# Fire attention: weights, transposes and output steps moved to later slots of the pipeline

## The chip, the cores and the metric

The kernel runs on one core of a Trainium2 chip. A core has five engines that run side by side and are tied together only by semaphores: TensorE (PE: matmuls; PEld is its loading of stationary operands), VectorE (DVE), ScalarE (ACT), GpSimd (POOL) and SyncE (SP, which issues transfers). The metric is the device time of one execution in microseconds; less is better.

## The reference

The reference runs two layers of a "macaron" network on x of 8 x 256 tokens with 128 channels, in float32: a mixture of experts, a gated linear recurrence and the mixture again, then six layers of local attention, one attention with a FIRE position bias, and the six local layers again. Each part starts from a layer norm and its output is added to x. The change touches the FIRE attention alone:

```python
qkv = x @ Wqkv + bqkv
q, k, v = jnp.split(qkv, 3, axis=-1)      # 16 heads of 8 channels each
bias = fire_bias(T, w1, b1, w2, b2, c_param, L_multiplier)   # (1, 16, T, T), -inf above the diagonal
att = jnp.einsum('bhqd,bhkd->bhqk', q, k) * scale + bias
att = jax.nn.softmax(att, axis=-1)
y = jnp.einsum('bhqk,bhkd->bhqd', att, v)
return y.transpose(0, 2, 1, 3).reshape(B, T, C) @ Wproj + bproj
```

## The kernel before

Every phase is written engine by engine: each engine has its own program, executes it strictly in the order written, and waits on semaphores where it needs another engine's result. The phase in question is `fire_attention_phase`. Its first blocks load the constants, build the position bias of both query tiles and the projections q, k, v of the eight batches. Its last block, the attention proper, is what the change rewrites.

The attention is cut into 96 **items**, 12 for each of 8 batches. An item q is one PSUM bank of 128 x 512 scores. Items 0 to 3 of a batch are the first 128 queries: 4 heads by 128 keys each. Items 4 to 11 are the other 128 queries: 2 heads by 256 keys. Items 3 and 11 of a batch end an output **tile** of 128 queries, so there are 16 tiles. Each item goes through these steps:

- `scores` (PE, L1564): four matmuls at once, one for each of the next four items, into banks 0 to 3. Before the next four it waits until the bias has been added to all earlier items (`addd`).
- `add_bias` (DVE, L1663), four in a row as soon as the scores are there, into one of eight buffers S (traced as fa_nd); then `maximum` (DVE, L1670), one a slot.
- subtraction of the maximum (POOL, L1544), in place.
- exponential (ACT, L1639), in place.
- `turn_weights` (PE, L1555): four 128 x 128 transposes into bank 4 or 5, and their copy to pT (ACT, L1633). There are three buffers pT.
- `weigh` (PE, L1592): four matmuls with the values into bank 6 or 7, whose column of ones also gives the sum of the softmax.

A finished tile then takes: copy of heads (ACT, L1627, oh), `turn_heads` (PE, L1580, four transposes), `take_output` (DVE, L1675 and L1679: reciprocal and product, on), `turn_output` (PE, L1575), its copy (ACT, L1645, oT), `project` (PE, L1570), its copy with the bias (ACT, L1651, ysb) and `update` (DVE, L1685, M += ysb).

The order on each engine comes from a software pipeline. The loop `stream` counts slots n, and in slot n an engine does a step for item n - k if the step has lag k:

```python
SIM, PTR, PVS, OTT, OTR, YPR = 0, 2, 3, 4, 5, 6
def stream(slot):
    for n in range(GN + YPR):
        slot(n)
```

So PE's slot n is: turn_weights(n - 2), scores(n) if n is a multiple of 4, project of the tile that ended at n - 6, turn_output (n - 5), turn_heads (n - 4), weigh(n - 3). ACT's slot n is: heads (n - 4), pT (n - 2), exponential of item n, oT (n - 5), ysb (n - 6). DVE's slot n is: four add_bias if n is a multiple of 4, maximum(n), take_output (n - 4), update (n - 6). An exponential is thus written two slots ahead of its transposes. The phase has no loop on the chip and its attention block issues no transfers.

Of the kernel before, what the change touches and what calls it, by code (L numbers as in the profile page):

```python
# [9 lines left out]
ACT = mybir.ActivationFunctionType  # L10
AX = mybir.AxisListType

P = 128
# [1302 lines left out]
def fire_attention_phase(nc, res, d, M, XN):  # L1316

    bank, ident = res["bank"], res["ident"]
# [3 lines left out]
    GN = B * GB  # L1322
    RM = T + 4 * (T // 4 - 1)
    ROFF = RM - T
    with ExitStack() as ctx:
        phase = res["phase"] = res["phase"] + 1

        def sb(name, shape, dt=FP32):
            return ctx.enter_context(nc.sbuf_tensor(f"{name}_{phase}", shape, dt))

        def sem(name):
            s = ctx.enter_context(nc.semaphore(f"{name}_{phase}"))
            sems.append(s)
            return s
        sems = []
        wqkv, wp = sb("fa_wqkv", [P, C]), sb("fa_wp", [P, P])
        bqk, bv = sb("fa_bqk", [P, 3]), sb("fa_bv", [P, P])
# [9 lines left out]
        bias = [sb("fa_bias0", [P, NH, P]), sb("fa_bias1", [P, NH, T])]  # L1347
# [4 lines left out]
        S = nd[:, :, :, :].rearrange("p a i n -> p (a i n)").rearrange("p (g n) -> p g n", g=8)  # L1352
        mx = sb("fa_mx", [P, 8, GR])
        pT = sb("fa_pT", [P, 3, 4, P])
        rd = sb("fa_rd", [P, 2, NH])
        on = sb("fa_on", [P, 2, P])
        oh = sb("fa_oh", [P, 2, 512])
        oT = sb("fa_oT", [P, 2, P])
        ysb = sb("fa_ysb", [P, 2, P])
# [3 lines left out]
        simd, addd, mxd, subd, expd = [sem("fa_" + n) for n in ("simd", "addd", "mxd", "subd", "expd")]  # L1363
        ptT, ptE, pvd = [sem("fa_" + n) for n in ("ptT", "ptE", "pvd")]
        ohE, ohT, rdd, ond, oTd, oTe, yd, yE, upd = [sem("fa_" + n) for n in (
            "ohE", "ohT", "rdd", "ond", "oTd", "oTe", "yd", "yE", "upd")]
        SCALE = float(np.float32(1.0) / np.sqrt(np.float32(HD)))

        with nc.Block() as block:
            @block.sync  # L1370
            def _(sp):
                for dst, src in ((sc[:, 0:2], d["fa_sc"].to_broadcast([P, 2])), (rel[:, :], d["c_rel"]), (pn[:, :], d["c_pos"]),
                                 (wb[:, :], d["fa_wb"]), (wqkv[:, :], d["fa_wqkv"]), (bqk[:, :], d["fa_bqk"]),
                                 (bv[:, :], d["fa_bv"].to_broadcast([P, P])), (b2[:, :], d["fa_b2"].to_broadcast([P, NH])),
                                 (hmask[:, :], d["c_hmask"]), (wp[:, :], d["fa_wp"])):
                    sp.dma_start(dst, src).then_inc(ld, 16)
                sp.wait_ge(zd, 1)
                for g in range(4):
                    sp.dma_start(w2[g * BW:(g + 1) * BW, g * NH:(g + 1) * NH], d["fa_w2"]).then_inc(ld, 16)
                sp.wait_ge(ld, 16 * 14)  # L1380
# [129 lines left out]
                    spread_keys(r)  # L1510
                    forget_future(r)

        SIM, PTR, PVS, OTT, OTR, YPR = 0, 2, 3, 4, 5, 6

        def at(n, k):

            return n - k if 0 <= n - k < GN else None

        def info(q):

            b, i = divmod(q, GB)
            part, r = divmod(i, GR)
            return (b, r, 0, 0, 4, P) if part == 0 else (b, r, 1, 2 * (part - 1), 2, T)

        def tile_end(q):

            if q is None or q % GB not in (GR - 1, GB - 1):
                return None
            return 2 * (q // GB) + (q % GB == GB - 1)

        def stream(slot):
            for n in range(GN + YPR):
                slot(n)

        with nc.Block() as block:
# [13 lines left out]
            def _(pe):  # L1549
# [47 lines left out]
                def slot(n):  # L1597
# [16 lines left out]
                    if q is not None:  # L1614
                        weigh(q)
                stream(slot)

            @block.scalar
            def _(act):
                def slot(n):  # L1620
                    qe = at(n, OTT)
                    tl = tile_end(qe)
                    if tl is not None:
                        act.wait_ge(pvd, qe + 1)
                        if tl >= 2:
                            act.wait_ge(ohT, tl - 1)
                        nc.scalar.activation(oh[:, tl % 2, :], bank[6 + tl % 2][:, :], ACT.Copy).then_inc(ohE, 1)  # L1627
                    q = at(n, PTR)
                    if q is not None:
                        act.wait_ge(ptT, q + 1)  # L1630
                        if q >= 3:
                            act.wait_ge(pvd, q - 2)
                        nc.scalar.activation(pT[:, q % 3, :, :], bank[4 + q % 2][:, :].rearrange("p (h q) -> p h q", h=4),  # L1633
                                             ACT.Copy).then_inc(ptE, 1)
                    q = at(n, SIM)
                    if q is not None:
                        act.wait_ge(subd, q + 1)
                        s = S[:, q % 8, :]
                        nc.scalar.activation(s, s, ACT.Exp).then_inc(expd, 1)  # L1639
                    tl = tile_end(at(n, OTR))  # L1640
                    if tl is not None:
                        act.wait_ge(oTd, tl + 1)
                        if tl >= 2:
                            act.wait_ge(yd, tl - 1)
                        nc.scalar.activation(oT[:, tl % 2, :], bank[6 + tl % 2][:, 0:P], ACT.Copy).then_inc(oTe, 1)  # L1645
                    tl = tile_end(at(n, YPR))
                    if tl is not None:
                        act.wait_ge(yd, tl + 1)
                        if tl >= 2:
                            act.wait_ge(upd, tl - 1)  # L1650
                        nc.scalar.activation(ysb[:, tl % 2, :], bank[6 + tl % 2][:, P:2 * P], ACT.Identity,  # L1651
                                             bias=bqk[:, 2:3]).then_inc(yE, 1)
                stream(slot)

            @block.vector
            def _(dve):
                def add_bias(q):
                    _, r, t, a, nh, nk = info(q)
                    s = S[:, q % 8, :].rearrange("p (h k) -> p h k", h=nh)
                    dve.wait_ge(simd, q + 1)  # L1660
                    if q >= 8:
                        dve.wait_ge(ptT, q - 7)
                    nc.vector.tensor_tensor(s, bank[r][:, :].rearrange("p (h k) -> p h k", h=nh),  # L1663
                                            bias[t][:, 4 * r + a:4 * r + a + nh, 0:nk], ALU.add).then_inc(addd, 1)

                def maximum(q):
                    _, _, _, _, nh, nk = info(q)
                    s = S[:, q % 8, :].rearrange("p (h k) -> p h k", h=nh)
                    dve.wait_ge(addd, q + 1)
                    nc.vector.tensor_reduce(mx[:, q % 8, 0:nh], s, AX.X, ALU.max).then_inc(mxd, 1)  # L1670

                def take_output(tl):
                    o = bank[6 + tl % 2][:, :].rearrange("p (h c) -> p h c", h=NH)
                    dve.wait_ge(ohT, tl + 1)
                    nc.vector.reciprocal(rd[:, tl % 2, :], o[:, :, HD]).then_inc(rdd, 1)  # L1675
                    dve.wait_ge(rdd, tl + 1)
                    if tl >= 2:
                        dve.wait_ge(oTd, tl - 1)
                    nc.vector.tensor_tensor(on[:, tl % 2, :].rearrange("p (h c) -> p h c", h=NH), o[:, :, 0:HD],  # L1679
                                            rd[:, tl % 2, :].unsqueeze(2).to_broadcast([P, NH, HD]), ALU.mult).then_inc(ond, 1)  # L1680

                def update(tl):
                    m = M[:, tl * P:(tl + 1) * P]
                    dve.wait_ge(yE, tl + 1)
                    nc.vector.tensor_tensor(m, m, ysb[:, tl % 2, :], ALU.add).then_inc(upd, 1)  # L1685

                def slot(n):
                    q = at(n, SIM)
                    if q is not None:
                        if q % GR == 0:  # L1690
                            for k in range(GR):
                                add_bias(q + k)
                        maximum(q)
                    tl = tile_end(at(n, OTT))
                    if tl is not None:
                        take_output(tl)
                    tl = tile_end(at(n, YPR))
                    if tl is not None:
                        update(tl)
                stream(slot)  # L1700
        clear(nc, sems)


def program(nc, d, out):
    with ExitStack() as ctx:
# [48 lines left out]
        local_transformer_phase(nc, res, d, X)  # L1754
        layer_norm_block(nc, res, M, plain(XN), add_shifted=X)
        fire_attention_phase(nc, res, d, M, XN)
        layer_norm_block(nc, res, M, shifted(X))
        local_transformer_phase(nc, res, d, X)
# [92 lines left out]
```

## Time and profile before

| what | value |
|---|---|
| median of three executions | 4402.37 us (4397.21 to 4403.71) |
| the profiled execution | 4395.94 us, span 4394.2 us |
| granted TensorE clock, mean of the span | 0.936 of full |
| busy in the span | PE 3849.0, DVE 3408.9, ACT 3185.7, PEld 2781.2, POOL 2692.8 us |
| attention block of the FIRE phase | 2392.26 to 2697.67 us of the span |

The span is the time from the first to the last instruction; 1.7 us of the execution lie around it. The full clock is 2.4 GHz and the row of the clock knows one other level here, 0.50 or 1.2 GHz; a value between is a stretch with both. Most of the span is the two stages of local attention. The attention block is 7% of it.

### The profile page before, as it was taken

To read this page: it belongs to the slowest core of one execution; us is meant where nothing else is said; L and a number is where in the kernel's file an instruction comes from. 1 tells how busy PE (TensorE), PEld (TensorE's weight loads), DVE (VectorE), ACT (ScalarE), POOL (GpSimd) and SP (SyncE) were. 2 spreads that over 40 slices of the span, in tenths; PEclk is the share of its full clock that TensorE was granted. 3 is DMA by queue.
4 is the path that set the end of the run, shared out by engine and by line. 5 is a ranking of instruction groups with operands and counts; after the bars stand their busy time and mean duration, and the time that the engine had idled before them with its cause. 6 is when DMAs were issued, how large, how long until landed. Compare 5 with 4: busy or idle time off the path is not lost. (4 is left out here: it accounts for less than half of the span.)

```text
span 4394.2 us, 163943 instructions
## 1 busy us (share of the span) xinstructions
PE 3849.0 (88%) x64208; PEld 2781.2 (63%) x64208; DVE 3408.9 (78%) x6643; ACT 3185.7 (72%) x10371; POOL 2692.8 (61%) x2514
## 2 busy tenths in 40 slices
PE   7966968999999999999966665899999999999996
PEld 3423427777777777777745443777777777777773
DVE  1122129999999999999945444999999999999994
ACT  3443437888888888888843433788888888888884
POOL 1110128777777777777723332778777777877772
PEclk8987989999999999999976776999999999999997
DMA  1101113333333333333310000333333333333331
GB/s 58 58 15 44 58 47 103 114 103 117 102 117 104 104 117 105 115 96 109 117 33 7 1 1 33 103 118 103 116 100 117 103 107 114 104 117 96 109 117 39
DMA packets 549312, 377.94 MB, mean 86 GB/s; under 512 B 32576, under 2 KB 533056, under 8 KB 546240
## 3 DMA queue, kind: packets, MB, share of 16 engines
q1 hardware_dynamic: 548560, 367.57, 27.8%
q8 instruction: 514, 8.42, 0.8%
q14 instruction: 238, 1.95, 0.1%
HBM read 265.37 MB, written 102.11 MB: 84 GB/s over the span
## 5 line engine op out<-in xcount | busy, mean ns | idle before, releaser
L1266 POOL TENSOR_TENSOR lt_t<-lt_t 128x512 f32<-128x512 f32 x768 | 973.4, 1289 | 566.9 <-DVE lt_t L1100 566.9
L1002 ACT ACTIVATE lt_pb<-lt_pb,lt_mx 128x64 f32<-128x64 f32 x3072 | 1023.7, 346 | 0.0
L1272 POOL TENSOR_TENSOR lt_t<-lt_t,lt_rn 128x512 f32<-128x512 f32 x768 | 810.9, 1076 | 116.9 <-DVE lt_rn L1128 115.6
L49 PE MATMUL ps<-lt_wh,lt_xh 128*128 128x512 f32 (+1 forms) x1536 | 580.2, 378 | 150.5 <-DVE lt_t L1100 88.7
L1002 ACT ACTIVATION_READ_ACCUMULATOR lt_pb<-lt_pb,lt_mx 128x1 f32 x3072 | 611.5, 199 | 0.0
L984 ACT ACTIVATE lt_qkT<-ps 128x512 f32<-128x512 f32 x768 | 459.0, 598 | 196.5 <-PE ps L804 196.1
L1111 DVE TENSOR_REDUCE lt_ss<-lt_sq 128x8 f32<-128x512 f32 x768 | 518.3, 675 | 14.1 <-ACT lt_sq L979 10.1
L1100 DVE TENSOR_TENSOR lt_t<-ps,lt_tab 128x512 f32<-128x512 f32 x768 | 522.3, 680 | 2.9
L1106 DVE TENSOR_TENSOR lt_t<-ps,lt_tab 128x512 f32<-128x512 f32 x768 | 520.9, 678 | 2.1 <-PE ps L804 0.8
L51 PE MATMUL ps<-lt_wh,lt_xl 128*128 128x512 f32 (+1 forms) x1536 | 522.4, 340 | 0.0
L50 PE MATMUL ps<-lt_wl,lt_xh 128*128 128x512 f32 (+1 forms) x1536 | 521.0, 339 | 0.0
L804 PE MATMUL ps<-ident,lt_t 128*128 128x128 f32 x3072 | 482.1, 280 | 35.1 <-ACT lt_qkT L984 25.4
L979 ACT ACTIVATE lt_sq<-ps 128x512 f32<-128x512 f32 x768 | 452.5, 589 | 69.2 <-PE ps L51 68.6
L49 PEld LDWEIGHTS ps<-lt_wh,lt_xh 128*128 128x128 f32 x1536 | 289.6, 189 | 269.5 <-issue 151.5
L804 PEld LDWEIGHTS ps<-ident,lt_t 128*128 128x128 f32 x3072 | 355.4, 141 | 160.2 <-issue 106.7
L862 PEld LDWEIGHTS ps<-lt_pT,lt_vw 64*64 64x64 f32 x24576 | 398.0, 135 | 88.3 <-issue 88.0
L862 PE MATMUL ps<-lt_pT,lt_vw 64*64 64x32 f32 x24576 | 440.0, 221 | 3.1 <-issue 3.1
L1278 POOL TENSOR_TENSOR lt_pb<-lt_pb,lt_rd 128x512 f32<-128x512 f32 x384 | 400.6, 1043 | 29.9 <-DVE lt_rd L1145 26.9
L876 PE MATMUL ps<-lt_oT,lt_wo 128*128 128x256 f32 x1536 | 405.0, 386 | 1.4 <-ACT lt_oT L1014 1.4
L372 POOL TENSOR_TENSOR M<-M,moe_tmp 128x512 f32<-128x512 f32 x64 | 80.9, 1264 | 511.2 <-DVE moe_tmp L354 511.2
L354 DVE SCALAR_TENSOR_TENSOR moe_tmp<-ps,moe_bb,moe_cbc 128x512 f32<-128x512 f32 x64 | 48.0, 750 | 421.4 <-PE ps L306 421.4
L832 PEld LDWEIGHTS ps<-lt_qkT 64*32 64x32 f32 x24576 | 270.1, 105 | 136.2 <-issue 133.7
(200 smaller groups left out, 7823.6 us busy)
## 6 DMA issues: line engine op xcount, KB each, us to landing
lt_vw<-v_scratch SPq DMA_DIRECT2D x768, 256.0 KB, 3.8
v_scratch<-lt_vv SPq DMA_DIRECT2D x384, 256.0 KB, 2.1
lt_wraw<-in_lt_wqkv SPq DMA_DIRECT2D x56, 384.0 KB, 5.7
moe_cbc<-comb_scratch SPq DMA_DIRECT2D x16, 1024.0 KB, 6.5
moe_w<-in_moe_w SPq DMA_DIRECT2D x32, 256.0 KB, 2.8
lt_wo<-in_lt_wo SPq DMA_DIRECT2D x48, 128.0 KB, 3.7
lt_w<-in_lt_w SPq DMA_DIRECT2D x12, 341.0 KB, 4.5
lt_w<-in_lt_w SPq DMA_DIRECT2D x12, 192.0 KB, 4.1
```

The lines of the kernel that those rows point to most:

```text
L49: nc.tensor.matmul(out, lh, rh, start=start, stop=False)
L50: nc.tensor.matmul(out, lh, rl, start=False, stop=False)
L51: return nc.tensor.matmul(out, ll, rh, start=False, stop=stop)
L804: ins = nc.tensor.transpose(TB[:, q * P:(q + 1) * P], t1[:, u[1] % 2, t, q * P:(q + 1) * P], ident[:, :])
L862: ins = nc.tensor.matmul(OR[r][64 * e:64 * e + 64, t * P + w * WIN:t * P + w * WIN + WIN], vw[h, k, 4 * t + w, e * DH:(e + 1) * DH], pT[h, ...
L984: nc.scalar.activation(qkT[:, u[1] % 2, :, WIN + t * P:WIN + (t + 1) * P], TB.rearrange("p (a n) -> p a n", a=4), ACT.Copy).then_inc(tE[t], 1)
L1002: ins = nc.scalar.activation(p, p, ACT.Exp, bias=mx[:, par, c:c + 1], accum_out=sm[:, par, c:c + 1])
L1100: nc.vector.tensor_tensor(o4, a4[:, :, :, ::-1, :], s4, ALU.mult).then_inc(rotd[t], 1)
L1106: nc.vector.tensor_tensor(t1[:, u[1] % 2, t, :].rearrange("p (w h c) -> p w h c", w=2, c=DH), A[t][:, :].rearrange("p (w h c) -> p w h c", ...
L1111: nc.vector.tensor_reduce(ss[:, u[1] % 2, 8 * t:8 * t + 8], sq[:, t, :].rearrange("p (h c) -> p h c", c=DH), AX.X, ALU.add).then_inc(ssd[t ...
L1266: nc.gpsimd.tensor_tensor(o, o, t2[:, t, :], ALU.add).then_inc(padd[t], 1)
L1272: nc.gpsimd.tensor_tensor(o, o, rn[:, u[1] % 2, 8 * t:8 * t + 8].unsqueeze(2).to_broadcast([P, 8, DH]), ALU.mult).then_inc(qkd[t], 1)
```

## The change

The lags become SIM 0, EXP 3, PTR 5, PVS 6, OEV 7, OTT 8, OTR 9, YPR 10, UPD 11. The exponential, the copy of heads and the update get lags of their own. The transposes keep two slots from the exponential, but the exponential now stands three slots behind scores, maximum and subtraction. In ScalarE's slot it moves to the end, behind the copies oT and ysb. VectorE's slot now begins with take_output and update, and the bias and maximum follow. The loop runs 11 slots past the last item in place of 6. No instruction is added or removed, and no shape changes; the steps themselves become functions.

```diff
--- before.py
+++ after.py
@@ -1510,7 +1510,7 @@
                     spread_keys(r)
                     forget_future(r)
 
-        SIM, PTR, PVS, OTT, OTR, YPR = 0, 2, 3, 4, 5, 6
+        SIM, EXP, PTR, PVS, OEV, OTT, OTR, YPR, UPD = 0, 3, 5, 6, 7, 8, 9, 10, 11
 
         def at(n, k):
 
@@ -1529,7 +1529,7 @@
             return 2 * (q // GB) + (q % GB == GB - 1)
 
         def stream(slot):
-            for n in range(GN + YPR):
+            for n in range(GN + UPD):
                 slot(n)
 
         with nc.Block() as block:
@@ -1617,39 +1617,54 @@
 
             @block.scalar
             def _(act):
+                def take_heads(q, tl):
+                    act.wait_ge(pvd, q + 1)
+                    if tl >= 2:
+                        act.wait_ge(ohT, tl - 1)
+                    nc.scalar.activation(oh[:, tl % 2, :], bank[6 + tl % 2][:, :], ACT.Copy).then_inc(ohE, 1)
+
+                def take_weights(q):
+                    act.wait_ge(ptT, q + 1)
+                    if q >= 3:
+                        act.wait_ge(pvd, q - 2)
+                    nc.scalar.activation(pT[:, q % 3, :, :], bank[4 + q % 2][:, :].rearrange("p (h q) -> p h q", h=4),
+                                         ACT.Copy).then_inc(ptE, 1)
+
+                def exponential(q):
+                    act.wait_ge(subd, q + 1)
+                    s = S[:, q % 8, :]
+                    nc.scalar.activation(s, s, ACT.Exp).then_inc(expd, 1)
+
+                def take_output(tl):
+                    act.wait_ge(oTd, tl + 1)
+                    if tl >= 2:
+                        act.wait_ge(yd, tl - 1)
+                    nc.scalar.activation(oT[:, tl % 2, :], bank[6 + tl % 2][:, 0:P], ACT.Copy).then_inc(oTe, 1)
+
+                def take_result(tl):
+                    act.wait_ge(yd, tl + 1)
+                    if tl >= 2:
+                        act.wait_ge(upd, tl - 1)
+                    nc.scalar.activation(ysb[:, tl % 2, :], bank[6 + tl % 2][:, P:2 * P], ACT.Identity,
+                                         bias=bqk[:, 2:3]).then_inc(yE, 1)
+
                 def slot(n):
-                    qe = at(n, OTT)
-                    tl = tile_end(qe)
+                    q = at(n, OEV)
+                    tl = tile_end(q)
                     if tl is not None:
-                        act.wait_ge(pvd, qe + 1)
-                        if tl >= 2:
-                            act.wait_ge(ohT, tl - 1)
-                        nc.scalar.activation(oh[:, tl % 2, :], bank[6 + tl % 2][:, :], ACT.Copy).then_inc(ohE, 1)
+                        take_heads(q, tl)
                     q = at(n, PTR)
                     if q is not None:
-                        act.wait_ge(ptT, q + 1)
-                        if q >= 3:
-                            act.wait_ge(pvd, q - 2)
-                        nc.scalar.activation(pT[:, q % 3, :, :], bank[4 + q % 2][:, :].rearrange("p (h q) -> p h q", h=4),
-                                             ACT.Copy).then_inc(ptE, 1)
-                    q = at(n, SIM)
-                    if q is not None:
-                        act.wait_ge(subd, q + 1)
-                        s = S[:, q % 8, :]
-                        nc.scalar.activation(s, s, ACT.Exp).then_inc(expd, 1)
+                        take_weights(q)
                     tl = tile_end(at(n, OTR))
                     if tl is not None:
-                        act.wait_ge(oTd, tl + 1)
-                        if tl >= 2:
-                            act.wait_ge(yd, tl - 1)
-                        nc.scalar.activation(oT[:, tl % 2, :], bank[6 + tl % 2][:, 0:P], ACT.Copy).then_inc(oTe, 1)
+                        take_output(tl)
                     tl = tile_end(at(n, YPR))
                     if tl is not None:
-                        act.wait_ge(yd, tl + 1)
-                        if tl >= 2:
-                            act.wait_ge(upd, tl - 1)
-                        nc.scalar.activation(ysb[:, tl % 2, :], bank[6 + tl % 2][:, P:2 * P], ACT.Identity,
-                                             bias=bqk[:, 2:3]).then_inc(yE, 1)
+                        take_result(tl)
+                    q = at(n, EXP)
+                    if q is not None:
+                        exponential(q)
                 stream(slot)
 
             @block.vector
@@ -1685,18 +1700,18 @@
                     nc.vector.tensor_tensor(m, m, ysb[:, tl % 2, :], ALU.add).then_inc(upd, 1)
 
                 def slot(n):
+                    tl = tile_end(at(n, OTR))
+                    if tl is not None:
+                        take_output(tl)
+                    tl = tile_end(at(n, UPD))
+                    if tl is not None:
+                        update(tl)
                     q = at(n, SIM)
                     if q is not None:
                         if q % GR == 0:
                             for k in range(GR):
                                 add_bias(q + k)
                         maximum(q)
-                    tl = tile_end(at(n, OTT))
-                    if tl is not None:
-                        take_output(tl)
-                    tl = tile_end(at(n, YPR))
-                    if tl is not None:
-                        update(tl)
                 stream(slot)
         clear(nc, sems)
```

TensorE at the beginning of the attention block (L1564 scores, L1555 transposes, L1592 product with the values), before:

```order
L1564 MATMUL ps<-fa_kz,fa_qT 128x512 x4
L1555 MATMUL ps<-ident,fa_nd 128x128 x8
L1592 MATMUL ps<-fa_pT,fa_vv 32x128 x4
L1555 MATMUL ps<-ident,fa_nd 128x128 x4
L1564 MATMUL ps<-fa_kz,fa_qT 128x512 x4
```

and now:

```order
L1564 MATMUL ps<-fa_kz,fa_qT 128x512 x8
L1555 MATMUL ps<-ident,fa_nd 128x128 x8
L1592 MATMUL ps<-fa_pT,fa_vv 32x128 x4
L1555 MATMUL ps<-ident,fa_nd 128x128 x4
L1592 MATMUL ps<-fa_pT,fa_vv 32x128 x4
L1555 MATMUL ps<-ident,fa_nd 128x128 x4
L1564 MATMUL ps<-fa_kz,fa_qT 128x512 x4
```

The second four scores (x8 is two groups of four) now stand ahead of the first transposes, where they stood behind the third item's; and from there on a group of scores always stands three items earlier in the row of transposes.

ScalarE around the end of the first tile, from its copy of heads (fa_oh) to its copy of the result (fa_ysb), before:

```order
L1627 ACTIVATE fa_oh<-ps 128x512
L1633 ACTIVATE fa_pT<-ps 128x512
L1639 ACTIVATE fa_nd<-fa_nd 128x512
L1633 ACTIVATE fa_pT<-ps 128x512
L1639 ACTIVATE fa_nd<-fa_nd 128x512
L1645 ACTIVATE fa_oT<-ps 128x128
L1633 ACTIVATE fa_pT<-ps 128x512
L1639 ACTIVATE fa_nd<-fa_nd 128x512
L1651 ACTIVATE fa_ysb<-ps,fa_bqk 128x128
```

and now (L1624 heads, L1630 pT, L1636 exponential, L1642 oT, L1648 ysb):

```order
L1624 ACTIVATE fa_oh<-ps 128x512
L1630 ACTIVATE fa_pT<-ps 128x512
L1636 ACTIVATE fa_nd<-fa_nd 128x512
L1630 ACTIVATE fa_pT<-ps 128x512
L1636 ACTIVATE fa_nd<-fa_nd 128x512
L1630 ACTIVATE fa_pT<-ps 128x512
L1642 ACTIVATE fa_oT<-ps 128x128
L1636 ACTIVATE fa_nd<-fa_nd 128x512
L1630 ACTIVATE fa_pT<-ps 128x512
L1648 ACTIVATE fa_ysb<-ps,fa_bqk 128x128
L1636 ACTIVATE fa_nd<-fa_nd 128x512
```

Between the copy of heads and the copy of the output there are now three copies of weights in place of two, and oT and ysb stand ahead of their slot's exponential, no longer behind it.

## Rows read from the trace of the kernel before

**Rows 1.** Busy time by stretch: attention block, half clock, full clock, idle, afterwards, local attention
```profile
core 0: us, PE busy (x) PEld busy (x) DVE busy (x) ACT busy (x) POOL busy (x), PEclk, DMA share, GB/s
2392.20:2697.70 305.50, 212.01 (x1456) 122.45 (x1456) 129.98 (x240) 121.88 (x240) 97.34 (x96) 0.72 0.00 1
2459.80:2464.60 4.80, 4.78 (x26) 3.05 (x26) 1.48 (x3) 2.35 (x5) 2.18 (x3) 0.50 0.01 3
2465.00:2468.70 3.70, 3.70 (x40) 1.97 (x34) 1.66 (x3) 1.46 (x3) 0.00 (x0) 1.00 0.00 0
2468.80:2471.80 3.00, 0.00 (x0) 0.00 (x0) 3.00 (x6) 0.53 (x1) 1.60 (x2) 0.98 0.00 0
2471.90:2474.90 3.00, 2.95 (x16) 2.12 (x17) 0.00 (x0) 2.61 (x6) 2.33 (x3) 0.50 0.00 0
3200.00:3300.00 100.00, 93.42 (x1929) 73.27 (x1930) 98.44 (x189) 86.86 (x310) 81.43 (x76) 1.00 0.35 103
```

**Rows 2.** Waits of TensorE in the block: total us, times, longest
```profile
PE ps L1570 <- ACT fa_oT L1645: 57.0, 16, 3.9
PE ps L1555 <- ACT fa_nd L1639: 31.1, 9, 4.9
```

**Rows 3.** Timeline of one group of four items: start us, length us, engine, line
```profile
2428.19 1.14 PE L1564 MATMUL ps<-fa_kz,fa_qT 32*128 32x512 f32 x8
...
2429.26 0.63 PE L1592 MATMUL ps<-fa_pT,fa_vv 128*32 128x128 f32 x8
2429.35 2.48 DVE L1663 TENSOR_TENSOR fa_nd<-ps,fa_bias 128x512 f32<-128x512 f32 x4 [4.63 <-PE ps L1564]
...
2429.83 0.66 PE L1555 MATMUL ps<-ident,fa_nd 128*128 128x128 f32 x4
...
2430.41 0.63 PE L1592 MATMUL ps<-fa_pT,fa_vv 128*32 128x128 f32 x8
2431.75 2.45 DVE L1670 TENSOR_REDUCE fa_mx<-fa_nd 128x4 f32<-128x512 f32 x4
2432.51 4.03 POOL L1544 TENSOR_TENSOR fa_nd<-fa_nd,fa_mx 128x512 f32<-128x512 f32 x4 [6.26 <-DVE fa_mx L1670]
2433.58 0.63 ACT L1639 ACTIVATE fa_nd<-fa_nd 128x512 f32<-128x512 f32 x1 [4.68 <-POOL fa_nd L1544]
...
2434.26 1.12 PE L1555 MATMUL ps<-ident,fa_nd 128*128 128x128 f32 x4 [3.22 <-ACT fa_nd L1639]
```

**Rows 4.** Timeline of TensorE at full clock, items of the first 128 queries
```profile
2475.55 0.43 PE L1592 MATMUL ps<-fa_pT,fa_vv 128*32 128x128 f32 x8
2475.90 0.66 PE L1555 MATMUL ps<-ident,fa_nd 128*128 128x128 f32 x4
2476.49 1.14 PE L1564 MATMUL ps<-fa_kz,fa_qT 32*128 32x512 f32 x8
2477.56 0.33 PE L1575 MATMUL ps<-ident,fa_on 128*128 128x128 f32 x1
2477.82 0.42 PE L1592 MATMUL ps<-fa_pT,fa_vv 128*32 128x128 f32 x8
```

**Rows 5.** Timeline of TensorE at half clock
```profile
2488.21 1.07 PE L1592 MATMUL ps<-fa_pT,fa_vv 128*32 128x128 f32 x8
2489.21 1.12 PE L1555 MATMUL ps<-ident,fa_nd 128*128 128x128 f32 x4
2490.26 2.07 PE L1564 MATMUL ps<-fa_kz,fa_qT 32*128 32x512 f32 x8
2492.26 0.33 PE L1575 MATMUL ps<-ident,fa_on 128*128 128x128 f32 x1
```

**Rows 6.** Timeline: the block's first scores, its last products and its last update
```profile
2392.26 2.09 PE L1564 MATMUL ps<-fa_kz,fa_qT 32*128 32x512 f32 x8 [1.93 <-PEq L1414]
...
2692.35 1.39 PE L1592 MATMUL ps<-fa_pT,fa_vv 128*32 128x128 f32 x16
...
2697.38 0.29 DVE L1685 TENSOR_TENSOR M<-M,fa_ysb 128x128 f32<-128x128 f32 x1 [1.68 <-ACT fa_ysb L1651]
```

## The prediction

> **What bounds the kernel now.** I read first the busy times by stretch. The attention block takes 305.5 us and no engine fills it: PE 212.0, DVE 130.0, ACT 121.9, POOL 97.3 [rows 1]. PE is idle for 93.5 us, and PE's clock is at 0.72 of full, so a part of its busy time is slow work. The table of waits says where the idle time is: 57.0 us ahead of the 16 projections (waiting for the copy oT) and 31.1 us in 9 waits ahead of transposes (waiting for an exponential) [rows 2], 88.1 of the 93.5 us. Both are the same gap. The timeline of one group of four items shows it [rows 3]: adds from 2429.35, first maximum 2431.75, first subtraction 2432.51, first exponential 2433.58, its transposes 2434.26. From the adds to the first transposes of the same items there are 4.91 us; PE has only two products and one transposition left (to 2430.98) and then stands still for 3.22 us. At a tile's end it is oT that waits, because it stands in ACT's queue behind that exponential. So the cycle of a group is serial: scores, four adds, maximum, subtraction, exponential, then nearly all of PE's work for the group. It takes 305.4 / 24 = 12.7 us.
>
> The third thing to see is the clock. In a stretch in which PE worked without a gap it was 0.50 at first (2459.8 to 2464.6) and 1.00 after it (2465.0 to 2468.7). In the idle stretch behind it fell at the end (0.98 in the mean), and the next work ran at 0.50 [rows 1]. Each group pays the gap and then the half clock that follows it.
>
> **The change.** It removes and adds no instruction. It moves the exponential three slots behind the scores and everything after it by three to five slots. PE now issues scores of group g+1 behind the transposes of the last item of group g-1, not behind those of the third item of group g. The 4.91 us of adds, maximum, subtraction and exponential for group g+1 thus run beside PE's work on group g. There are eight buffers S: add_bias of item q waits for the transposes of item q-8, and for the last add of a group these stand in the same PE slot directly ahead of the scores that the add needs anyway. That costs nothing.
>
> *What PE needs if it never waits, at full clock.* Starts of neighbouring instructions: scores 2476.49 to 2477.56, 1.07 us; turn_output 0.26; product of an item of the first 128 queries 2475.55 to 2475.90, 0.35; its transposes 0.59 [rows 4]. Product of an item with 256 keys 2429.26 to 2429.83, 0.57; transposes 2429.83 to 2430.41, 0.58 [rows 3]. turn_heads has four transposes too: 0.58. The projection has no such row; it is one 128 x 128 product, so between turn_output (0.26) and the scores (1.07), nearest to the first: I take 0.35; the upper bound adds 0.7 x 16 = 11 us. One batch is 12 transpositions x 0.585 = 7.0, 8 products x 0.57 = 4.6, 4 x 0.35 = 1.4, 3 scores = 3.2, and 2 tiles x (0.58 + 0.26 + 0.35) = 2.4: 18.6 us, 6.2 a group.
>
> *Do the others keep up?* DVE needs, for a group, 2.40 us from the first add to the first maximum and 2.45 for four maxima [rows 3]; its whole busy time over the block is 130.0 us, 5.4 a group, below 6.2. ACT is at 121.9, 5.1 a group, POOL at 97.3, 4.1 [rows 1]. Their order: from A, the start of the adds, the exponential of a group's first item can start at A + 4.23 (2433.58 - 2429.35) and end at A + 4.86; its transposes stand in the slot behind the next scores, about A + 6.7 (6.2 and a product behind them). The fourth subtraction ends at A + 7.2 (2432.51 + 4.03), its transposes come three slots after those of the first, near A + 10. The exponential now stands behind oT and ysb and may be late by those, some 0.4 us, with over 1 us to spare. take_output stands ahead of the adds: its 0.6 us falls between turn_heads and the end of the next scores, in which PE has a product, a transposition and the scores (0.57 + 0.58 + 1.07). The update comes two slots later and no longer holds maxima up. The copy of heads stands a slot ahead of turn_heads. The closest race is ysb: the copy of result tl - 2 is in the slot right before the first product that needs its bank, about 1.5 us after the projection is issued; the copy takes about 1. For such joints I allow 3 us over the block.
>
> *Beginning and end.* First scores at half clock 2.1 us [rows 6], then 4.9 to the first transposes [rows 3]: 7.0. Four transpositions and two products, mostly at the half clock (1.05 and about 0.6), bring PE to the third scores at 12. From there to the 24th scores there are 21 groups x 6.2 = 130.2. Behind the start of the last scores come 1.07, 8 transpositions 4.7, 10 products 5.7 and a tile 1.2: 12.7. The last tile's chain from the end of the last product (2692.35 + 1.39) to the end of the last update (2697.67) is 3.9 [rows 6] and stays.
>
> Sum: 12 + 130.2 + 12.7 + 3.9 + 3 = 161.8 us against 305.4: 143.6 less. Everything outside the block is as before. The profiled execution took 4395.9, so 4252.3; it lies 6.4 below the median of the runs shown, and from the median the same sum gives 4258.8. I give the middle, 4255.
>
> **The clock, and a rule that speaks against this.** The full clock is granted in rows where PE did transposes for about half its time: 1.00 from 2465.0 to 2468.7, and 1.00 over 100 us of local attention in which PE was busy for 93.42 us [rows 1]. I therefore take the full clock. The Trainium skill (TensorE: Matmul & The Clock Gate, Part 4: PE-mode transpose) says that transposes don't count as busy for the gate, so that the full clock isn't reached with them; by that the block would go as in the first rival below. The rows speak against it, though none shows this mix at full clock for more than a few us.
>
> **The rivals.**
> *Half clock.* PE has no gap but the clock stays at 1.2 GHz. Then scores take 2.00, products 1.00 (the short ones about 0.6), transpositions 1.05, turn_output 0.26 [rows 5], and a tile about 2. A batch is 12.6 + 8 + 2.5 + 6 + 4 = 33.1, a group 11.0; 21 groups 231, beginning 13, end 22, chain 5: 271 us, 34 less than now, so 4365. For it: the block's clock is 0.72 today. Against: it was low behind gaps alone. Chance 0.07.
>
> *A wait in each group.* ACT's queue is strict: copy of weights, oT or ysb, exponential. For items of the first 128 queries PE's slot (0.35 + 0.58) is shorter than ACT's two activations (121.9 us of ACT for 96 items, 1.27 with the tile's), so PE waits there for pT; and DVE, at 5.4 of 6.2, has little reserve. If a group takes 6.9 to 7.5, 21 groups cost 15 to 27 us more: 4270 to 4282. Chance 0.15.
>
> *Another engine is the bound.* PE's weight loads fill only 1.97 of 3.70 us where the clock was full [rows 1]; if PE could pack its instructions closer than it did there, DVE would bind at 130.0 plus some 12 of beginning and end, 142 us: 4235. The Trainium skill (Perfetto Trace Analysis, Identifying the Most-Contended Engine) judges TensorE by its weight loads instead of its matmul rows, and by that DVE with 130.0 is the engine to watch, not PE with 122.45. But the steps of rows 3 and 4 are starts with nothing to wait for between them. Chance 0.04.
>
> *Slower: the copy of heads blocks ScalarE, at half clock.* It stands one slot behind its tile's last product, at the head of the slot, and everything on ACT queues behind it. If PE is at the half clock and this becomes serial, each tile pays product 1.07, copy of heads and copy of weights 0.6 each, exponential 0.63 and three hand-overs of 0.1, 3.2 us: 16 x 3.2 = 51, and 271 + 51 = 322 us, 17 more than now, 4415. It decides from 2.1 us a tile at half clock; at full clock it would need 9 us a tile and can't. Against: PE has a transposition of the next item to do in the meantime, and pT has three buffers. Chance 0.04.
>
> **How the numbers follow.** Forecast 0.70, with its own range 4243 to 4268 (the joints and the projection's price on one side, a DVE that hides all joints on the other, and the 6 us by which executions differ). The range given reaches over the waiting rival to 4284: 0.70 and most of 0.15. About 0.2% or 9 us is what can be told from no change. All cases but the last are faster by more: 0.96; the last 0.03 slower, and 0.01 for something that ends level.
>
> **What would show it.** In the new profile the block should take about 162 us; PE's waits for oT (57.0) and for exponentials (31.1) should all but vanish; PE's busy time should fall from 212 to near 150 with the clock near 1.00 after the first 11 us; DVE's waits for scores stay, now short (about 0.8 us a group). Transpositions should start every 1.15 us (0.93 for the first 128 queries), scores every 6.2. If the clock reads 0.50 with PE full, the first rival holds; if PE shows repeated waits for pT or for scores' banks with the clock at 1.00, the second; if the weight loads move closer than in rows 4, the third. The forecast is wrong if the block takes under 150 or over 180 us, or if anything outside it changes.

## The result and the profile after

| | before | changed |
|---|---|---|
| median of four executions | 4400.65 us | 4252.76 us (4244.38 to 4257.05) |
| ratio | | 0.9662 (0.9647 to 0.9676) |
| profiled execution, its span | 4395.94, 4394.2 us | 4251.9, 4250.1 us |
| attention block | 305.4 us | 156.0 us (2399.46 to 2555.46) |
| PE busy in the block | 212.0 us | 149.6 us |
| granted clock in the block | 0.72 | 0.96 |

The change makes the kernel 3.4% faster. The forecast of 4255 us and the reason given for it hold. Busy time by stretch of the changed kernel: the block, its first 12.4 us, the 21 groups from the third scores to the 24th, and one batch of 12 items from scores to scores. They answer to the first row of [rows 1]. In rows of TensorE, x counts records of the profile: four matmuls of scores, or four products with the values, stand as eight records, a projection as two.

```profile
core 0: us, PE busy (x) PEld busy (x) DVE busy (x) ACT busy (x) POOL busy (x), PEclk, DMA share, GB/s
2399.40:2555.50 156.10, 149.60 (x1456) 91.49 (x1456) 133.94 (x240) 120.21 (x240) 97.47 (x96) 0.96 0.01 2
2399.40:2411.80 12.40, 9.53 (x52) 4.37 (x52) 9.62 (x16) 4.50 (x8) 6.38 (x7) 0.50 0.00 1
2411.80:2538.00 126.20, 126.20 (x1276) 78.30 (x1279) 116.59 (x207) 104.10 (x208) 84.53 (x84) 1.00 0.01 2
2460.10:2478.10 18.00, 18.00 (x183) 11.19 (x182) 16.83 (x31) 14.95 (x31) 12.19 (x13) 1.00 0.01 2
```

From the third scores on PE is busy for 126.20 of 126.20 us at clock 1.00. One batch takes 18.00 us, with VectorE at 16.83. The waits of TensorE in the block, changed kernel (total us, times, longest), answer to [rows 2]:

```profile
PE ps L1564 <- DVE fa_nd L1678: 2.5, 1, 2.5
...
PE ps L1575 <- DVE fa_on L1694: 1.7, 2, 1.0
...
PE ps L1570 <- ACT fa_oT L1642: 0.4, 1, 0.4
PE ps L1555 <- ACT fa_nd L1636: 0.3, 1, 0.3
```

The 57.0 us for oT have become 0.4 and the 31.1 us for exponentials 0.3. (L1555 and L1564 are the same steps as before; oT is L1642 now, the exponential L1636, the update L1700, adds L1678, maximum L1685.) The timeline of one group in steady state, changed kernel, answers to [rows 3] (start us, length us, engine, line):

```profile
2460.11 1.14 PE L1564 MATMUL ps<-fa_kz,fa_qT 32*128 32x512 f32 x8
...
2461.26 2.48 DVE L1678 TENSOR_TENSOR fa_nd<-ps,fa_bias 128x512 f32<-128x512 f32 x4 [0.61 <-PE ps L1564]
...
2463.67 2.46 DVE L1685 TENSOR_REDUCE fa_mx<-fa_nd 128x2 f32<-128x512 f32 x4
...
2463.83 0.66 PE L1555 MATMUL ps<-ident,fa_nd 128*128 128x128 f32 x4
...
2464.32 0.60 PE L1580 MATMUL ps<-ident,fa_oh 128*128 128x128 f32 x4
...
2464.42 4.03 POOL L1544 TENSOR_TENSOR fa_nd<-fa_nd,fa_mx 128x512 f32<-128x512 f32 x4 [2.06 <-DVE fa_mx L1685]
...
2464.85 0.43 PE L1592 MATMUL ps<-fa_pT,fa_vv 128*32 128x128 f32 x8
...
2465.49 0.63 ACT L1636 ACTIVATE fa_nd<-fa_nd 128x512 f32<-128x512 f32 x1
...
2465.80 1.14 PE L1564 MATMUL ps<-fa_kz,fa_qT 32*128 32x512 f32 x8
```

The adds still start 1.15 us after the scores, the first subtraction comes 3.16 us after the adds and the exponential of the first item at 2465.49, 4.23 us after them, exactly the chain of before. But PE works through all of it and issues the next scores at 2465.80. The wait of the adds for the scores is what is left of VectorE's idle time, 12.5 us over the block.

Two more places of the changed kernel's timeline: PE at a projection, and an update on VectorE.

```profile
2467.48 0.66 PE L1555 MATMUL ps<-ident,fa_nd 128*128 128x128 f32 x4
...
2467.97 0.39 PE L1570 MATMUL ps<-fa_oT,fa_wp 128*128 128x128 f32 x2
...
2468.29 0.42 PE L1592 MATMUL ps<-fa_pT,fa_vv 128*32 128x128 f32 x8
...
2470.11 4.08 POOL L1544 TENSOR_TENSOR fa_nd<-fa_nd,fa_mx 128x512 f32<-128x512 f32 x4 [1.65 <-DVE fa_mx L1685]
...
2470.54 0.76 DVE L1700 TENSOR_TENSOR M<-M,fa_ysb 128x128 f32<-128x128 f32 x1
```

A projection costs 0.32 us (2467.97 to 2468.29), and the transposes directly ahead of it only 0.49. The update takes 0.76 us where it took 0.29 before; that was not foreseen.

Of the 149.4 us that the block lost, the profiled execution shows 144.0. Its code ahead of the block is the same, yet it took 7.2 us more (the block began at 2399.46 in place of 2392.26), and the code behind took 1.9 less. In other executions the block began anywhere from 2389.6 to 2400.6, so this is the scatter of the stages ahead of it. For the experiments the length of the block, from its first scores to the end of its last update, is therefore the better measure, and it stands first below.

### The profile page after: what moved, and what is told of

The parts are those of the page before. It is cut to its first block and busy times, and to the rows that moved or that the text cites. A ratio compares the mean times of both kernels' runs of the same rounds, so it can differ in the third digit from the quotient of the medians.

```text
span 4250.1 us, 163943 instructions
## 1 busy us (share of the span) xinstructions
PE 3795.4 (89%) x64208; PEld 2755.8 (65%) x64208; DVE 3413.5 (80%) x6643; ACT 3184.4 (75%) x10371; POOL 2693.3 (63%) x2514
## 5 line engine op out<-in xcount | busy, mean ns | idle before, releaser
L1111 DVE TENSOR_REDUCE lt_ss<-lt_sq 128x8 f32<-128x512 f32 x768 | 518.7, 675 | 14.3 <-ACT lt_sq L979 10.1
L333 ACT ACTIVATE moe_H<-ps,moe_bb 128x512 f32<-128x512 f32 x256 | 175.7, 687 | 250.1 <-PE ps L297 248.8
## 6 DMA issues: line engine op xcount, KB each, us to landing
lt_wo<-in_lt_wo SPq DMA_DIRECT2D x48, 128.0 KB, 3.8
```

What stands on the lines that cost most here:

```text
L1111: nc.vector.tensor_reduce(ss[:, u[1] % 2, 8 * t:8 * t + 8], sq[:, t, :].rearrange("p (h c) -> p h c", c=DH), AX.X, ALU.add).then_inc(ssd[t ...
```

## The experiments

Unless said otherwise each edit is made to the changed kernel; "block" is its length in the profile. Where no ratio is given the kernel was executed once; a total of one execution says little below some 10 us (the four of the changed kernel reach from 4244.38 to 4257.05), so the block counts there.

### The order inside the slots without the lags

```diff
-SIM, EXP, PTR, PVS, OEV, OTT, OTR, YPR, UPD = 0, 3, 5, 6, 7, 8, 9, 10, 11
+SIM, EXP, PTR, PVS, OEV, OTT, OTR, YPR, UPD = 0, 0, 2, 3, 4, 4, 5, 6, 6
```

> The changed order inside the slots (exponential last on ScalarE, output steps first on VectorE), but the lags of before. Theory (the gain is that scores are issued ahead of the transposes of the group before, so that adds, maximum, subtraction and exponential run beside TensorE's work): the serial chain of 4.9 us from the adds to the first transposes stays in each of the 24 groups, so most of the gain goes; oT no longer stands behind the exponential, which moves a projection and a product (some 1.3 us a tile at half clock) into the gap. Block 270 to 290 us, 4365 to 4385 in all. Rival (the 57 us of waits for oT were the cost, and the order inside the slots removed them): block under 230 us, under 4330.

Block 316.8 us, 4413.29 in all, ratio 1.0030 (1.0021 to 1.0040): 0.3% slower than before. The rival is out, but my own theory missed as well, by 27 us and in sign. The timeline of this kernel shows why:

```profile
2459.93 2.48 DVE L1678 TENSOR_TENSOR fa_nd<-ps,fa_bias 128x512 f32<-128x512 f32 x4 [2.93 <-PE ps L1564]
...
2462.34 0.68 DVE L1685 TENSOR_REDUCE fa_mx<-fa_nd 128x2 f32<-128x512 f32 x1
2463.09 1.04 POOL L1544 TENSOR_TENSOR fa_nd<-fa_nd,fa_mx 128x512 f32<-128x512 f32 x1 [8.04 <-DVE fa_mx L1685]
2464.16 0.63 ACT L1636 ACTIVATE fa_nd<-fa_nd 128x512 f32<-128x512 f32 x1 [3.68 <-POOL fa_nd L1544]
...
2465.18 0.36 ACT L1648 ACTIVATE fa_ysb<-ps,fa_bqk 128x128 f32<-128x128 f32 x1
...
2465.57 0.29 DVE L1700 TENSOR_TENSOR M<-M,fa_ysb 128x128 f32<-128x128 f32 x1 [2.56 <-ACT fa_ysb L1648]
2465.78 1.86 DVE L1685 TENSOR_REDUCE fa_mx<-fa_nd 128x2 f32<-128x512 f32 x3
2466.54 3.04 POOL L1544 TENSOR_TENSOR fa_nd<-fa_nd,fa_mx 128x512 f32<-128x512 f32 x3 [2.41 <-DVE fa_mx L1685]
```

The update waits for ysb, and ysb comes behind the group's first exponential. VectorE's new order puts the update ahead of the second maximum. So only one maximum is done when VectorE stops, and the subtractions of the other three items start at 2466.54, 3.45 us behind the first. In the kernel before, two maxima were done. PE's waits for exponentials, by far its largest here, are

```profile
PE ps L1555 <- ACT fa_nd L1636: 104.0, 39, 4.9
```

against 31.1 + 57.0 before.

### ScalarE's order alone

The lags as above, and VectorE's slot as before; only oT and ysb stand ahead of the exponential.

```diff
 # VectorE, on top of the lags above
-take_output at OTR, update at UPD, then adds and maximum
+adds and maximum, then take_output at OTT, update at YPR
```

> The lags and VectorE's order of before; only ScalarE's slot is changed (oT and ysb ahead of the exponential). It tells which half of the changed order made the order-only kernel slower. Theory (VectorE's new order puts the update, which waits for ysb, ahead of a group's second maximum in place of its third, so that three exponentials of the group instead of two are late): with VectorE's order of before the block falls below that of the order-only kernel (316.8 us) and below the 305.4 of before, since oT no longer waits behind the exponential: 280 to 300 us. Rival (it is ScalarE's order that costs: the ysb of a tile now stands behind the exponential of its slot before): block 310 us or more.

Block 283.1 us, 4379.11 in all, as expected. PE's waits for oT are down to 0.4 us, and those for exponentials are up from 31.1:

```profile
PE ps L1555 <- ACT fa_nd L1636: 76.6, 28, 4.9
```

So ScalarE's order is worth 22.3 us by itself, and VectorE's costs 33.7 on top of it (316.8 - 283.1), as long as the lags are the old ones.

### The lags without the order inside the slots

```diff
 # ScalarE
-heads (OEV), weights (PTR), oT (OTR), ysb (YPR), exponential (EXP)
+heads (OTT), weights (PTR), exponential (EXP), oT (OTR), ysb (YPR)
 # VectorE
-take_output (OTR), update (UPD), adds and maximum (SIM)
+adds and maximum (SIM), take_output (OTT), update (YPR)
```

> The new lags, but the order inside the slots of before: exponential ahead of oT and ysb, adds and maxima ahead of take_output and update, the copy of heads in the slot of its transposes, update in the slot of its projection. Theory (the lags are the gain): block 156 to 170 us; the copy of heads in the slot of turn_heads may cost TensorE up to 0.6 us a tile, 10 us in all. 4252 to 4268. Rival (the order inside the slots is the gain): block over 230 us, over 4330.

Block 167.1 us, ratio 0.9701 (0.9680 to 0.9722), as expected. The lags alone give 138.3 of the 149.4 us. The 11 us that are left are what the order adds once the lags are there. PE's waits in this kernel name a part of them:

```profile
PE ps L1580 <- ACT fa_oh L1624: 7.8, 16, 0.8
PE ps L1592 <- ACT fa_ysb L1648: 2.7, 7, 0.4
```

The copy of heads, now in the same slot as its transposes, costs 7.8 us in 16 waits, and the copy of the result, behind the exponential, 2.7. In the changed kernel these are 0.7 and nothing.

### Shorter lags

```diff
-EXP, PTR, PVS, OEV, OTT, OTR, YPR, UPD = 3, 5, 6, 7, 8, 9, 10, 11
+EXP, PTR, PVS, OEV, OTT, OTR, YPR, UPD = 2, 4, 5, 6, 7, 8, 9, 10    # two slots
+EXP, PTR, PVS, OEV, OTT, OTR, YPR, UPD = 1, 3, 4, 5, 6, 7, 8, 9     # one slot
```

> All lags from the exponential on one slot shorter (exponential two slots behind scores, transposes four). Theory: the first exponential of a group can start 4.2 us after the adds, and ScalarE's slot two behind the scores is reached after about 2.8 us, so it holds the copy of the next weights up; TensorE then waits 0.3 to 0.8 us a group, less 1.1 us for one slot less at the end: block 160 to 175 us. Rival (any lag that puts the scores ahead of the transposes is enough): block 155 us.

> All lags two slots shorter (exponential one slot behind scores, transposes three). Theory: scores are now issued behind the transposes of item 4g-3, those of items 4g-2 and 4g-1 remain as cover, 2.3 us at full clock against the chain of 4.9; TensorE waits about 1.5 to 2.5 us a group, and the clock may fall in some: block 195 to 250 us. Rival (any lag that puts the scores ahead is enough): block under 160 us.

Two slots: block 183.5 us, one slot: 224.6. Both rivals are out: putting the scores early is not enough. With two slots the loss (27.5 us) is larger than expected, and the waits of TensorE in that kernel show what I left out:

```profile
PE ps L1575 <- DVE fa_on L1694: 17.6, 16, 1.4
PE ps L1555 <- ACT fa_nd L1636: 10.1, 9, 4.9
```

One slot less shifts the output steps against the groups of four: take_output falls behind three maxima of VectorE instead of into its idle time ahead of the adds, and PE waits for it 1.1 us at each tile's end, 17.6 us in all where the changed kernel has 1.7. That is the larger part of the loss. Of the 10.1 us for exponentials 4.9 stand ahead of the block's first transposes; the second scores now come behind these, and the third scores start 15.7 us after the first and not 12.3. So only 5.2 us of the later waits are for a chain with too little cover. With one slot both waits are larger, and the clock is at 0.86 in the block:

```profile
PE ps L1575 <- DVE fa_on L1694: 26.1, 16, 1.9
PE ps L1555 <- ACT fa_nd L1636: 21.9, 9, 4.9
```

A lag here sets two things, the cover and the place within a group. Two slots with take_output left in its place, and four slots or more, were not run.

### The clock alone

The kernel before, with 24 transposes of the identity in each gap. Their result is overwritten by the transposes of the next item.

```diff
+                def fill(q):
+                    pe.wait_ge(ptE, q - 1)
+                    for _ in range(24):
+                        nc.tensor.transpose(bank[4 + q % 2][:, 0:P], ident[:, :], ident[:, :])
...
                         turn_weights(q)
+                    if n % GR == 1 and n > 1 and n < GN:
+                        fill(n - 1)
```

> The kernel before with 24 transposes of the identity put into each group's gap on TensorE (their result is overwritten by the transposes that follow). It tells how much of the gain is the clock. Theory (two thirds idle time, one third clock): the clock stays at 1.00, the serial chain stays, a group takes 4.9 us of chain plus 4.5 to 5 us of TensorE and scores, 9.4 to 10: block 230 to 245 us, 4325 to 4340. Rival (the whole gain is the clock, the gap only its cause): block 150 to 180 us. Second rival (the clock never mattered, the chain is all): block 300 us or more.

Block 279.4 us, 4376.96 in all. Busy time of two groups from scores to scores, and of the block:

```profile
core 0: us, PE busy (x) PEld busy (x) DVE busy (x) ACT busy (x) POOL busy (x), PEclk, DMA share, GB/s
2455.07:2475.95 20.88, 17.89 (x168) 12.76 (x167) 10.55 (x19) 9.51 (x19) 8.12 (x8) 1.00 0.00 1
2400.60:2680.00 279.40, 225.14 (x2008) 155.05 (x2008) 130.01 (x240) 119.48 (x240) 97.52 (x96) 0.94 0.00 1
```

The clock is 1.00 over the two groups and 0.94 over the block, and the block is 26 us shorter, where I had expected 60 to 75. Both rivals are out (the clock as the whole gain, and a clock that never mattered); the clock matters, but less than in my theory. The filler itself does not hold the groups up: in each of the 23 gaps its last transpose ends 0.3 to 1.3 us before the exponential for which the next transposes wait. A group still takes 10.4 us in the stretch shown (20.88 for two), 11.6 in the mean. The chain of VectorE, GpSimd and ScalarE sets it, and the update's wait for ysb is still in it (41.5 us of VectorE's idle time). A faster PE hardly shortens a cycle that waits for other engines.

### TensorE as the bound

```diff
-                    for h in range(4):
+                    for h in (0, 1, 2, 3, 0, 1, 2, 3):
```

> The changed kernel with each item's four transposes issued twice (same result). Theory (TensorE is the bound, without waits): each item costs 0.49 to 0.58 us more, 96 of them 47 to 56: block 203 to 213 us. Rival (VectorE or ScalarE binds, TensorE has room): under 180 us.

Block 195.1 us, 39.1 more, and PE's busy time rises by nearly the same, 40.1 (149.6 to 189.7). Each item costs 0.41 us more and not 0.49 to 0.58: eight transposes in a row take 1.02 us in that profile, to the next scores, where four take 0.58:

```profile
2461.98 1.09 PE L1555 MATMUL ps<-ident,fa_nd 128*128 128x128 f32 x8
2463.00 1.14 PE L1564 MATMUL ps<-fa_kz,fa_qT 32*128 32x512 f32 x8
```

The size was missed, the kind was not.

### VectorE's room

```diff
+        mx2 = sb("fa_mx2", [P, GN // GR, GR])
...
+                    if q % GR == GR - 1:
+                        nc.vector.tensor_reduce(mx2[:, q // GR, 0:nh], s, AX.X, ALU.max)
```

> The changed kernel with one more maximum on VectorE in each group (its result goes to a buffer that nothing reads), 0.61 us a group, 14.7 us of work. Theory (TensorE is the bound and VectorE has 18.0 - 16.8 = 1.2 us a batch to spare by its busy time): most of the room is used up; 1.83 us more a batch against 1.2: block 156 to 163 us. Rival (VectorE is as much the bound as TensorE): block 170 us.

Block 160.4 us: of 12.8 us more busy time of VectorE (133.94 to 146.69) 4.4 reach the end. TensorE's waits for take_output are 6.3 us, where the changed kernel has 1.7:

```profile
PE ps L1576 <- DVE fa_on L1697: 6.3, 16, 1.4
```

VectorE is close behind TensorE but not the bound.

### The update moved to where GpSimd is idle

```diff
-YPR, UPD = 10, 11
+YPR, UPD = 10, 13
 # VectorE
-take_output, update, adds, maximum
+take_output, adds, update, maximum
```

> The changed kernel with the update M += ysb moved two slots later and between the adds and the first maximum, where GpSimd has nothing to subtract. Theory (the update took 0.76 us in place of 0.29 because a subtraction ran on GpSimd at the same time): the 16 updates fall back to 0.29, VectorE's busy time falls by some 6 us, and the block stays at 156 us because TensorE is the bound. Rival (it is slower because of where M or ysb come from): 0.76 stays.

Timeline of this kernel, with the scores that bound one batch:

```profile
2461.57 1.14 PE L1564 MATMUL ps<-fa_kz,fa_qT 32*128 32x512 f32 x8
...
2471.31 0.28 DVE L1700 TENSOR_TENSOR M<-M,fa_ysb 128x128 f32<-128x128 f32 x1
...
2472.26 4.04 POOL L1544 TENSOR_TENSOR fa_nd<-fa_nd,fa_mx 128x512 f32<-128x512 f32 x4 [2.34 <-DVE fa_mx L1685]
...
2479.58 1.14 PE L1564 MATMUL ps<-fa_kz,fa_qT 32*128 32x512 f32 x8
```

The updates take 0.28 us in the median and VectorE's busy time falls from 133.9 to 128.0 us. A batch takes 18.01 us, the same as the 18.00 of the changed kernel. The block reads 153.7 us, 2.3 less. Of this 1.9 is a clock that rose earlier: the third scores start 10.9 us after the first, not 12.3, and the fourth 5.7 after them, not 6.2. This is not the edit's doing, since the first update comes later than that; and the changed kernel, executed once more below, shows 11.8 and 5.7. The other 0.4 us lie behind the last scores. The total was 4248.37 in one execution, which tells nothing at this size.

### A try to get below: transposes of two items together

On top of the kernel with the moved update:

```diff
-                    q = at(n, PTR)
-                    if q is not None:
-                        turn_weights(q)
+                    if n % 2:
+                        for q in (at(n, PTR), at(n, PTR - 1)):
+                            if q is not None:
+                                turn_weights(q)
```

> The kernel with the update moved, and on TensorE the transposes of two items together in every odd slot. Theory (TensorE is the bound, and transposes behind transposes take 0.44 to 0.49 us in place of 0.58): 48 x 0.1 to 0.14 = 5 to 7 us less: block 147 to 151 us, 0.1 to 0.2% of the whole. Rival (products behind products, or waits for pT, give it back): block 154 to 160 us.

> The changed kernel as it is, on the same chip as the pairs, for comparison: block 154 to 157 us, ratio to before 0.965 to 0.968.

The pairs: block 167.6 us, ratio 0.9690 (0.9676 to 0.9703). The changed kernel again: block 155.0 us, ratio 0.9648 (0.9634 to 0.9661). The pairs are slower, and by more than theory and rival had. They do save PE time, 143.9 us busy against 148.6, but PE now waits for exponentials:

```profile
PE ps L1555 <- ACT fa_nd L1637: 17.2, 32, 0.8
```

The second transposes of each pair stand one slot earlier than before, so the distance to their exponential is one slot where it was two. 17.2 us of waits outweigh 4.6 us of saved work. No version tried is clearly below the change: the block with the moved update, 153.7 us, differs from the 155.0 and 156.0 of the change by little more than these do from each other.

## Why the prediction was right

**What bounded the kernel.** The serial chain per group was the right reading. Taking it away by the lags alone gives 138.3 of 149.4 us; ScalarE's order alone, which frees oT, gives 22.3. The step "both are the same gap" holds: freeing oT moved most of the wait to the exponentials (31.1 to 76.6 us).

**The sum.** Term by term: beginning 12 us, measured 12.3; 21 groups 130.2, measured 126.1 (2411.76 to 2537.82); from the last scores to the last product's end 12.7, measured 13.7, with 1.0 in it of a wait for take_output that the sum did not have; the last chain 3.9, measured 3.9 (2551.52 to 2555.46); joints 3, measured none. Together 161.8 against 156.0. The group came out at 6.0 us and not 6.2 because steps beside other transposes are cheaper than I priced them: turn_heads and the transposes ahead of it took 1.02 us (2463.83 to 2464.85) and not 1.17, the projection and the transposes ahead of it 0.81 and not 0.94; in both it is above all the transposes ahead, at 0.49 in place of 0.58. That is 0.28 us a tile, 0.56 of the 18.6 a batch.

**The number.** 4255 against 4252.76 is closer than the sum was. The block was 5.8 us shorter than forecast, and in the profiled execution the stages around it were 5.3 us longer than in that of before. The two misses cancel there. That is luck, and the range was made for it.

**The clock.** It rose while the third scores ran and was at 1.00 to the end of the groups, with PE on transposes for about half its time (55.2 us for the weights and 12.7 for heads and outputs, of 126.2). The prediction read as much out of two rows of the kernel before, and wrongly: there transposes were 1.31 of 3.70 us, and 22.9 of 100 us in local attention. So the full clock was right, but the rows behind it were weaker than it said. The Trainium skill's rule (TensorE: Matmul & The Clock Gate, Part 4: PE-mode transpose) that transposes don't count for the gate, as the prediction took it, would have kept it at half; the trace disagrees, 1.00 over 126.2 us. The filler says more, since it is nothing but transposes: with 24 of them in the gap the clock stayed at 1.00 over the two groups shown, where the empty gap had brought it to 0.50. What I had not worked out is how little the clock is worth by itself. With the gap filled by idle work it gives 26 us. In the changed kernel it should matter more, since PE is the bound there: by the rival's sum, an estimate, the same schedule at half clock would take 271 us. That schedule was not run at half clock.

**The other engines.** VectorE keeps up, but with less room than its 5.4 us a group suggested: the 16 updates took 11.2 us in place of 4.7 and its busy time rose by 4.0, and with one more maximum a group PE begins to wait. ScalarE keeps up as laid out: PE waited for it for 1.4 us in the whole block.

**The rule on weight loads.** The Trainium skill (Perfetto Trace Analysis, Identifying the Most-Contended Engine) judges TensorE by its weight loads, and by its share of the peak, which was not worked out here. The weight loads fill 78.3 of 126.2 us, below VectorE's 116.6, and yet twice the transposes moved the end by nearly all their time (39.1 of 40.1 us) and one more maximum a group by a third of its own (4.4 of 12.8). Here the matmul rows named the bound and the weight loads did not. (Twice the transposes is twice their weight loads as well, so the run shows that TensorE is the bound, and not which of its two parts is.)

**The rivals.** Half clock, VectorE as the bound and the slow copy of heads are all excluded by the rows above: the clock is 1.00, one more maximum costs 4.4 us and twice the transposes 39.1, and PE waits 0.7 us for the copy of heads in the whole block. A wait in each group did not appear with three slots of lag (126.20 of 126.20 us busy).

## What to carry to other kernels

In a pipeline written out by hand, look for the engine that has work and stands behind a chain of others; give the steps of that chain enough slots that the engine's own work for the items before covers them, and count the slots: here 4.9 us of chain lie hidden behind three. Look then at where the other steps come to stand: with two slots the block took 27.5 us more, and most of that was not the chain, but an output step that had slipped behind three maxima. The order inside a slot and the lags are not separable: an order that is right with the new lags was worse than nothing with the old ones, because it put a wait one instruction further ahead in a queue. An idle gap and the slow clock behind it look like two costs, but filling the gap with idle work gives back little where other engines set the cycle.

## What was not expected of the hardware

The update M += ysb on VectorE, with both inputs and the output in SBUF, takes 0.76 us (14 of 16 times) while GpSimd subtracts, and 0.29 us when GpSimd is idle. Moved to a place without a subtraction it is back at 0.28. What it loses depends on where in a subtraction it starts. Started 0.43 us into one it takes 0.76 us; 0.66 us into one (the kernel with one slot) 0.53; 0.11 us into one (a single update of the kernel with the update moved) 1.08. In all three it ends 0.15 us behind the end of that subtraction, as if it had waited for it. Started 0.16 us ahead of a subtraction (the kernel with two slots) it keeps its 0.28. Maxima, which have one input, take 0.68 us a piece in the median with a subtraction beside them (58 in the changed kernel) and without one (23). The Trainium skill (SBUF — State Buffer, Who interferes with whom) says that VectorE instructions with two SBUF inputs contend with GpSimd's reads and that reductions never do; the rows agree in both. The slower updates had no effect on the end, since TensorE was the bound (18.00 and 18.01 us a batch).

Eight transposes in a row take 1.02 us and four 0.58, and four ahead of another kind of transposes or a projection 0.49: the price of a short row of instructions on TensorE depends on what follows it, by about 0.1 us.
